# A GNN layer with experts followed by graph attention on one core: the MoE rounds run in teams of two groups of nodes instead of four, and the rows of x are fetched between the rounds, kept in memory and loaded back

## The chip, the core and the metric

The kernel runs on one core of a Trainium2 chip. The metric is the device time of one launch in microseconds (us); lower is better. One profiled execution shows what every engine did: TensorE (PE, with its weight loads as PEld), VectorE (DVE), ScalarE (ACT), GpSimd (POOL) and SyncE (SP), and the transfers of the DMA queues.

## The reference

The graph has 6250 nodes with 128 features (x) and 106,250 directed edges (50,000 pairs in both directions, and a self loop for each node). Everything is float32.

```
h = x @ W_in + b_in                                        # 6250 x 256
for l in 0, 1, 2:
    agg    = mean of h[src] over the edges that end in the node
    logits = [h, agg] @ router_W[l] + router_b[l]          # 8 experts
    gates  = softmax over the two largest logits, 0 elsewhere
    weak   = relu(agg @ weak_W[l][e] + weak_b[l][e])       # 4 experts, 256 -> 256
    strong = relu(agg @ W1[l][e] + b1) @ W2[l][e] + b2     # 4 experts, 256 -> 512 -> 256
    h      = h + sigmoid(h @ conf_W[l] + conf_b[l]) * sum_e gates[e] * expert_e
x = layernorm(x + h @ W_out + b_out)
y = elu(gat(x, 4 heads of 32)); x = layernorm(x + gat(y, 1 head of 128))
```

A gat layer adds up the rows of the neighbours with softmax weights that come from one score of the source and one of the destination for each head.

## The kernel before, in words

**Stages.** The kernel first sorts the nodes by degree, puts them into 49 groups of 128, computes h and gathers it in that order (up to about 330 us). Then come the three MoE rounds, then the normalised x is stored as the table for the first attention layer, and two attention layers follow. The change touches the three rounds, what lies between them, and the end of the sorting.

**Gathers.** In each round GpSimd issues 800 indirect gathers (`hidden_rows`, L589), each of 128 rows of h out of the round's table `hidden_tab[r]` in memory, one row for each node of a group. They go into a ring of 32 slots, which is used as 8 units of 4 slots. Before the third gather of a unit GpSimd waits until VectorE has freed the next unit (`ring_free`). SyncE loads the lists of row numbers for 32 gathers ahead (`stage`, L404 to L426) and tells VectorE unit by unit what has arrived (`tell`, L408 to L415).

**VectorE.** `aggregate(r, q, j)` (L875 to L901) adds up the units of group j of team q: it multiplies the first unit into the accumulator (L880), adds whole units (L886), adds the last one (L890), the node's own row and the sum over the four parts, and writes the mean into the team's aggregate (L901). For the first group of a team this write waits until TensorE has turned the aggregate of the team before (`tr_ready`), since there is one such buffer. A team is `TEAM` = 4 groups: 12 teams and a last one with a single group, 13 in all (`BATCHES`). VectorE's step of a team is an order written out by hand: the next team's aggregates one by one, and between them `rank_experts` (top two and what the exponential needs), `weigh_experts` (L957 on, the gates), and the adding of weak and strong experts to h (`add_weak`, L930; `add_strong`, L921).

**TensorE.** Its step of a team is written out too (`step` below): turn the aggregate (`turn_agg`, transposes), the router's product, computed as logits by nodes and turned back (`router`, `turn_logits`, L1668), the first layer of the strong experts (`strong_first`, L1677, four chunks of 128 outputs each, 512 columns for four groups), the weak experts of one group (L1687 with the bias, L1689), the second strong layer (`second`, L1700 with the bias, L1702, 256 columns for each group), and so on for the four experts and groups. The last second layer of a team comes at the start of the next team's step. In round 2 each step also turns the finished state of the team before and multiplies it by W_out (`turn_state`, `project`). At the start of each round a pass of 13 batches turns h and makes the part of the logits that depends on h itself (`own_turn`, `own_logits`, L1629 and L1640).

**ScalarE** copies the turned aggregate, does the relus (L1343) and the exponential (`gate_exp`, L1334), scales weak and strong results by the gates (L1364, L1352), and issues the store of a finished team's h into the next round's table (`keep_state`, L1376). The next round's first gather waits for all these stores (`table_done`).

**Weights.** One set of buffers serves all rounds. SyncE issues the loads of a round (L440 to L445) after it has told of the first 32 gathers of the round and when the second layers of the round before have ended; TensorE waits for `s_wts` ahead of the first step.

**x.** After the gathers of round 2 GpSimd fetches the 49 groups of x into a part of the ring (L626), when the ring is free. VectorE adds them to the projected state (`residual`, L986 to L993), takes the variances (L998), and ScalarE copies the turned result for the attention tables (L1451).

**Compaction.** At the end of the sorting the neighbours' numbers of each group are copied to their place in one list, group after group: VectorE one group (L841), ScalarE the next (L1293), in turn. SyncE stores the list (`slot_tab`) and loads its first 32 columns (L426); then GpSimd starts the first round (it waits for the list at L577).

## Time and profile before

| | us |
|---|---|
| runs | 5852.50, 5852.51, 5859.92; median 5852.51 |
| profiled execution, its own time | 5857.3 |
| its span | 5855.7 |
| GpSimd busy | 4188.6 (72%) |
| VectorE busy | 3452.8 (59%) |
| TensorE busy | 3218.5 (55%) |
| ScalarE busy | 1199.8 (20%) |
| sorting, h, up to the first gather | 330 |
| MoE rounds 0, 1, 2, first to last gather | 1017, 1015, 1037 |
| last gather of a round to the first of the next stage | 91, 89, 142 |
| rest: two attention layers and the output | 2134 |

The busy times are shares of the whole span. The stages differ in what limits them, so a share of 72% says little about any one of them; the rows below are read stage by stage.

### The profile page before, as it was taken

To read this page: it belongs to the slowest core of one execution; us is meant where nothing else is said; L and a number is where in the kernel's file an instruction comes from. 1 tells how busy PE (TensorE), PEld (TensorE's weight loads), DVE (VectorE), ACT (ScalarE), POOL (GpSimd) and SP (SyncE) were. 2 spreads that over 40 slices of the span, in tenths; PEclk is the share of its full clock that TensorE was granted. 3 is DMA by queue.
4 is the path that set the end of the run, shared out by engine and by line. 5 is a ranking of instruction groups with operands and counts; after the bars stand their busy time and mean duration, and the time that the engine had idled before them with its cause. 6 is when DMAs were issued, how large, how long until landed. Compare 5 with 4: busy or idle time off the path is not lost.

```text
span 5855.7 us, 59691 instructions
## 1 busy us (share of the span) xinstructions
PE 3218.5 (55%) x11995; PEld 2032.2 (35%) x11995; DVE 3452.8 (59%) x6754; ACT 1199.8 (20%) x2737; POOL 4188.6 (72%) x4323
## 2 busy tenths in 40 slices
PE   4068889999879899989899999200000000000000
PEld 3055555556545555565465566200000000000000
DVE  5337667674556666636566665555555556556563
ACT  1022223333223233323233333200000000000000
POOL 7777777772777777547777766477777767777777
PEclk8569999999889999979999999655555555555555
DMA  4144443441443333333333332223222222222221
GB/s 111 51 147 109 112 112 106 111 110 50 141 111 112 108 111 110 87 107 104 102 102 100 102 95 70 54 59 60 59 60 59 59 46 56 55 55 55 56 55 50
DMA packets 248524, 500.35 MB, mean 85 GB/s; under 512 B 103196, under 2 KB 132437, under 8 KB 248037
## 3 DMA queue, kind: packets, MB, share of 16 engines
q0 software_dynamic: 176592, 446.04, 29.5%
q1 hardware_dynamic: 55226, 33.55, 2.2%
q10 hardware_dynamic: 16608, 19.67, 1.0%
q8 instruction: 36, 0.59, 0.0%
q14 instruction: 62, 0.50, 0.0%
HBM read 464.23 MB, written 34.72 MB: 85 GB/s over the span
## 4 chain that ended last, share of the span: by engine, by line
POOL 25%; PE 24%; issue 15%; DVE 13%; DVEq 12%; DMA 6%; ACT 2%; ACTq 0%; POOLq 0%; SPq 0%
POOL ring L589 22%; PE ps_w1a L1677 5%; PE ps_w1b L1677 4%; PE ps_gate L1702 4%; PE ps_wide L1702 3%; DMA ring<-gat_tab,stage 3%; DVE ps_wide L1135 3%; PE ps_weak_a L1689 2%; PE ps_weak_b L1689 2%; DMA ring<-hidden_tab,stage 2%; DVEq L1167 2%; DVEq L883 1%; DVE ps_wide L930 1%; DVEq L1177 1%; DVEq L1180 1%
## 5 line engine op out<-in xcount | busy, mean ns | idle before, releaser
L589 POOL DMA_INDIRECT ring<-hidden_tab,stage x2400 | 2304.8, 960 | 954.4 <-issue 891.1
L589 POOL DMA_INDIRECT ring<-gat_tab,stage x1600 | 1543.6, 965 | 585.9 <-issue 545.1
L886 DVE TENSOR_TENSOR ps_wide<-ps_wide,ring 128x1024 f32<-128x1024 f32 x450 | 560.2, 1245 | 208.7 <-SPq L415 124.6
L1677 PE MATMUL ps_w1a<-agg_team_t,wbuf 128*128 128x512 f32 (+1 forms) x1248 | 562.2, 573 | 7.3 <-ACT strong L1343 5.9
L1702 PE MATMUL ps_gate<-wbuf,strong 128*128 128x256 f32 x2400 | 560.0, 380 | 0.0
L1677 PE MATMUL ps_w1b<-agg_team_t,wbuf 128*128 128x512 f32 (+1 forms) x1248 | 556.1, 568 | 0.0
L1807 PE MATMUL ps_w1a<-ident,agg_team_t 128*128 128x128 f32 x28 | 7.8, 434 | 995.9 <-DVE agg_team_t L1213 995.9
L1702 PE MATMUL ps_wide<-wbuf,strong 128*128 128x256 f32 x2304 | 537.3, 380 | 0.0
L1702 PEld LDWEIGHTS ps_gate<-wbuf,strong 128*128 128x128 f32 x2400 | 433.3, 191 | 110.6 <-issue 47.7
L1702 PEld LDWEIGHTS ps_wide<-wbuf,strong 128*128 128x128 f32 x2304 | 416.0, 191 | 77.9
L1495 ACT ACTIVATE ps_gate<-shifted 128x36 f32<-128x36 f32 x296 | 60.4, 204 | 1862.4 <-DVEq L1124 1849.1
L1141 DVE TENSOR_REDUCE h_res<-ps_wide 128x1188 f32 (+1 forms) x296 | 411.0, 1388 | 0.1
L930 DVE TENSOR_REDUCE ps_wide<-weak 128x256 f32<-128x1024 f32 x147 | 285.0, 1939 | 185.1 <-ACT weak L1364 171.6
L1135 DVE TENSOR_TENSOR ps_wide<-ring,ps_gate 128x1056 f32<-128x1056 f32 x296 | 372.9, 1260 | 0.0
L1343 ACT ACTIVATE strong<-ps_w1a,b_t 128x512 f32<-128x512 f32 (+1 forms) x312 | 206.7, 663 | 748.2 <-PE ps_w1a L1677 748.2
L1807 PEld LDWEIGHTS ps_w1a<-ident,agg_team_t 128*128 128x128 f32 x28 | 5.0, 217 | 998.0 <-DVE agg_team_t L1213 998.0
L890 DVE SCALAR_TENSOR_TENSOR ps_wide<-ring,before_cut,ps_wide 128x256 f32<-128x256 f32 x588 | 244.6, 485 | 174.8 <-SPq L415 136.3
L1677 PEld LDWEIGHTS ps_w1a<-agg_team_t,wbuf 128*128 128x128 f32 x1248 | 230.1, 191 | 306.3 <-issue 296.2
L1677 PEld LDWEIGHTS ps_w1b<-agg_team_t,wbuf 128*128 128x128 f32 x1248 | 231.9, 190 | 275.1 <-issue 275.1
L1107 DVE TENSOR_TENSOR score<-ring,h_res 128x32 f32 (+1 forms) x296 | 57.0, 193 | 443.0 <-SPq L419 386.2
L1689 PE MATMUL ps_weak_a<-wbuf,agg_team_t 128*128 128x512 f32 x588 | 289.1, 616 | 0.0
L1689 PE MATMUL ps_weak_b<-wbuf,agg_team_t 128*128 128x512 f32 x588 | 279.8, 599 | 0.0
(356 smaller groups left out, 4578.3 us busy)
## 6 DMA issues: line engine op xcount, KB each, us to landing
ring<-hidden_tab,stage POOLq DMA_INDIRECT x2400, 2.8
ring<-gat_tab,stage POOLq DMA_INDIRECT x1600, 2.6
hidden_tab<-h_res ACTq DMA_DIRECT2D x24, 512.0 KB, 3.0
hidden_tab<-h_res SPq DMA_DIRECT2D x12, 512.0 KB, 8.5
wbuf<-in_L_gnn_strong_W SPq DMA_DIRECT2D x6, 1024.0 KB, 9.5
wbuf<-in_L_gnn_strong_W SPq DMA_DIRECT2D x12, 512.0 KB, 14.3
gat_tab<-h_res ACTq DMA_DIRECT2D x7, 476.0 KB, 3.7
gat_tab<-h_res ACTq DMA_DIRECT2D x12, 272.0 KB, 2.4
```

Of the source, the lines that this page charges most:

```text
L589: return pool.indirect_dma_start(out=ring[:, b, 0:width], out_offset=None, in_=table, in_offset=bass.IndirectOffsetOnAxis(ap=stage[:, half ...
L886: nc.vector.tensor_tensor(wide_s, wide_s, rows(u), ALU.add).then_inc(ring_free, 1)
L890: nc.vector.scalar_tensor_tensor(wide_s[:, b, :], slot(last, b), before_cut[:, bass.ds(g + 1, 1), b:b + 1].rearrange("p a s -> p (a s)"), ...
L930: nc.vector.tensor_reduce(wide[:, 0:H], weak[j % 2][:].rearrange("p e n -> p n e"), AX.X, ALU.add)\
L1135: last = nc.vector.tensor_tensor(terms[:, 0:GSLOTS, :, :], rows_of(unit)[:, :, 0:HEADS * HC].rearrange("p s (h c) -> p s h c", c=HC), p[:, ...
L1141: nc.vector.tensor_reduce(sums(g), terms.rearrange("p s h c -> p (h c) s"), AX.X, ALU.add)
L1167: dve.drain()
L1343: nc.scalar.activation(strong[s % 2][:, c, 0:size * P], ps_w1[c % 2][:, 0:size * P], ACT.Relu, bias=b1_t[:, k:k + 1]).then_inc(relu_ready, 1)
L1495: nc.scalar.activation(ps_gate[:, 0:(GSLOTS + 1) * HEADS], shifted[:].rearrange("p s h -> p (s h)"), ACT.Exp).then_inc(p_ready, 1)
L1677: last = mm(ps_w1[c % 2][:, 0:size * P], w1_w[:, k, s, c * P:(c + 1) * P], agg_team_t[:, k, 0:size * P], start=k == 0, stop=k == 1)
L1689: last = mm(ps_weak[x][:], agg_team_t[:, k, j * P:(j + 1) * P], wk_w[:, k, x * 512:(x + 1) * 512], start=False, stop=k == 1)
L1702: last = mm(o, strong[s % 2][:, c, j * P:(j + 1) * P], w2_w[:, c, s, :], start=False, stop=c == 3)
```

## The change

- `TEAM` goes from 4 to 2: 24 teams and a last one with a single group, 25 turns. The batches of four stay for the projected state's residuals, the tables and the first pass of own logits. The rooms in SBUF and PSUM are cut anew: four buffers for the first layer's output (one for each strong expert) in place of two, two chunks of the first layer in one PSUM bank, and the state of the finished team in the upper half of `scaled_d`.
- The orders of a step on TensorE, VectorE and ScalarE are written anew. The exponential of the gates now stands on ScalarE behind all the relus of the team.
- The router's logits are made directly by nodes, with no turning back. Its bias comes in with the own logits by a product with a row of ones.
- The next round's own logits are made within the step, from the finished state of the team before (`turn_state` and `project` run in every round: logits in rounds 0 and 1, W_out in round 2). The pass of 13 batches stays ahead of round 0 alone and starts group by group as h lands.
- x is fetched by GpSimd in the passages: 32 groups after round 0, 17 after round 1. SyncE stores them in a table `x_tab` in five pieces, GpSimd waits for the stores before the next round's gathers, and SyncE loads all five pieces back into the ring after round 2.
- The compaction is done by VectorE alone with a drain behind each group.
- The bias parts in bf16 are computed across 128 partitions and brought into their rows through a table in memory; GpSimd no longer waits for them.

The core of the diff (left out are the counting of semaphores by turns instead of batches, the views of the new rooms, the helpers that follow the team's size, the bias parts and the first pass of own logits):

```
+X_PIECES = ((0, 8), (8, 20), (20, 32), (32, 44), (44, 49))
...
-TEAM = 4
+BATCHES = -(-GROUPS // BATCH)
+TEAM = 2
 TEAMS = GROUPS // TEAM
-BATCHES = TEAMS + 1
-STORES = 2 * BATCHES + BATCHES
+TURNS = TEAMS + 1
+PAIRS = 2
+STORES = 2 * TURNS + BATCHES
...
-EARLY = (TEAMS - 1) * TEAM
+EARLY = (BATCHES - 2) * BATCH
...
-strong = [sb(f"strong{i}", [P, 4, TEAM * P]) for i in range(2)]
+strong_room = sb("strong_room", [P, NS, 4, TEAM * P])
+strong = [strong_room[:, s, :, :] for s in range(NS)]
...
-scaled_d = sb("scaled_d", [P, TEAM, H])
-scaled = [scaled_a, scaled_b, scaled_c, scaled_d]
+scaled_d = sb("scaled_d", [P, BATCH, H])
+scaled = [scaled_a, scaled_b, scaled_c, scaled_d[:, 0:TEAM, :]]
+state_now = scaled_d[:, TEAM:2 * TEAM, :]
...
         if r == 1:
             keep_places(bodies - 1, bass.ds((bodies - 1) % 2 * RING, RING))
             sp.wait_ge(places_kept, bodies * 16 + 16)
+        if r in (1, 2):
+            for a, b in (X_PIECES[0:3], X_PIECES[3:])[r - 1]:
+                if a == 0:
+                    sp.wait_ge(ggathered[GUNITS - 1], 16 * GSLOTS)
+                else:
+                    sp.wait_ge(x_landed[(a - GSLOTS) // (3 * BATCH)], 16 * (b - a))
+                sp.dma_start(x_tab[:, a:b, :], x_ring[:, a:b, :]).then_inc(x_stored, 16)
+        if r == LAYERS:
+            sp.wait_ge(ring_free, bodies * (UNITS * LAYERS) + UNITS)
+            for c, (a, b) in enumerate(X_PIECES):
+                sp.dma_start(x_ring[:, a:b, :], x_tab[:, a:b, :]).then_inc(x_back[c], 16)
...
-    pool.wait_ge(s_strong_parts, 16 * len(PART_ROWS))
...
-        if r == LAYERS - 1:
-            pool.wait_ge(ring_free, bodies * (UNITS * LAYERS) + UNITS)
+        if r < 2:
+            pool.wait_ge(ring_free, bodies * (UNITS * (r + 1)) + UNITS)
             pool.sem_inc(half_begun, 1)
-            pool.wait_ge(agg_ready, LAYERS * BATCHES)
-            for g in range(GROUPS):
+            for g in (range(0, 32), range(32, GROUPS))[r]:
                 pool.indirect_dma_start(out=x_ring[:, g, :], out_offset=None, in_=x,
                                         in_offset=bass.IndirectOffsetOnAxis(ap=perm[:, g, 0:1], axis=0))\
-                    .then_inc(ggathered[GUNITS - 1] if g < GSLOTS else x_landed[(g - GSLOTS) // (3 * TEAM)], 16)
+                    .then_inc(ggathered[GUNITS - 1] if g < GSLOTS else x_landed[(g - GSLOTS) // (3 * BATCH)], 16)
+        if r < 2:
+            pool.wait_ge(x_stored, 16 * (3, len(X_PIECES))[r])
         if r < LAYERS - 1:
-            pool.wait_ge(table_done, 16 * BATCHES * (r + 1))
+            pool.wait_ge(table_done, 16 * TURNS * (r + 1))
...
     dve.wait_ge(s_blanked, 16)
-    def compact(g):
+    with dve.Fori(0, GROUPS) as g:
         at = dve.value_load(cum_at[0:1, bass.ds(g, 1)], min_val=0, max_val=COLS - RUN)
-        dve.wait_ge(s_compact, g + 1)
-        nc.vector.tensor_scalar(slots_sb[:, bass.ds(at, RUN)], run_raw[:, bass.ds(g, 1), :].rearrange("p a k -> p (a k)"),
-                                0.0, None, ALU.add).then_inc(s_compact, 1)
-    with dve.Fori(0, GROUPS // 2) as i:
-        compact(i * 2)
-    compact(GROUPS - 1)
+        nc.vector.tensor_scalar(slots_sb[:, bass.ds(at, RUN)], run_raw[:, bass.ds(g, 1), :].rearrange("p a k -> p (a k)"), 0.0, None, ALU.add)
+        dve.drain()
     dve.drain().then_inc(s_slots, 1)
...
         if j == 0:
-            w(dve, tr_ready, n * 2)
-        return nc.vector.tensor_scalar(agg4[:, j, :], part[:], rdeg[:, bass.ds(g, 1)], None, ALU.mult)
+            w(dve, tr_ready, n)
+        return nc.vector.tensor_scalar(agg_now[:, j, :], part[:], rdeg[:, bass.ds(g, 1)], None, ALU.mult)
...
-        if b < 2:
-            dve.wait_ge(ggathered[GUNITS - 1], 16 * GSLOTS)
-        else:
-            dve.wait_ge(x_landed[(b - 2) // 3], 16 * (3 * BATCH if b < TEAMS - 1 else 1 + BATCH))
-        dve.wait_ge(z_ready, b + 1)
+        dve.wait_ge(x_back[0 if b < 2 else min(1 + (b - 2) // 3, 4)], 16)
+        dve.wait_ge(z_ready, min((b + 1) * BATCH // TEAM, TURNS))
...
-            def between():
-                if r == LAYERS - 1 and spare:
-                    residual(spare.pop(0))
+            def between(count):
+                if r == LAYERS - 1:
+                    for _ in range(min(count, len(spare))):
+                        residual(spare.pop(0))
             spare = list(meanwhile)
             gather_next(0)
             if after == 1:
                 fill_up(r)
             if tail:
-                add_strong(r, q - 1, NS - 1, TEAM)
+                add_weak(r, q - 1, TEAM - 1, TEAM)
+                add_strong(r, q - 1, 2, TEAM)
+                add_strong(r, q - 1, 3, TEAM)
             rank_experts(r, q, size)
             weigh_experts(r, q, size)
+            between(2 if size == 1 else 0)
+            gather_next(1)
             add_weak(r, q, 0, size)
-            for s in range(1, NS):
-                gather_next(s)
-                between()
-                add_strong(r, q, s - 1, size)
-                between()
-                if s < size:
-                    dve.drain()
-                    add_weak(r, q, s, size)
+            add_strong(r, q, 0, size)
+            between(2 if size == 1 else 0)
+            add_strong(r, q, 1, size)
+            between(1)
         for j in range(TEAM):
             done = aggregate(r, 0, j)
...
         step(0, TEAM, TEAM, False)
         with dve.Fori(1, TEAMS - 1) as q:
             step(q, TEAM, TEAM)
-        step(TEAMS - 1, TEAM, 1, meanwhile=range(0, 6))
-        step(TEAMS, 1, 0, meanwhile=range(6, TEAMS))
+        step(TEAMS - 1, TEAM, 1, meanwhile=range(0, 1))
+        step(TEAMS, 1, 0, meanwhile=range(1, 6))
+        add_strong(r, TEAMS, 2, 1)
         if r == LAYERS - 1:
+            residual(6)
+        add_strong(r, TEAMS, 3, 1)
+        if r == LAYERS - 1:
+            for b in range(7, BATCHES - 1):
+                residual(b)
             variances(0, EARLY)
-        add_strong(r, TEAMS, NS - 1, 1)
...
-    act.wait_ge(s_cum, 1)
-    with act.Fori(0, GROUPS // 2) as i:
-        at = act.value_load(cum_at[0:1, bass.ds(i * 2 + 1, 1)], min_val=0, max_val=COLS - RUN)
-        act.wait_ge(s_compact, i * 2 + 2)
-        nc.scalar.activation(slots_sb[:, bass.ds(at, RUN)], run_raw[:, bass.ds(i * 2 + 1, 1), :].rearrange("p a k -> p (a k)"),
-                             ACT.Copy).then_inc(s_compact, 1)
...
-        def step(q, size, after, tail=True):
+        def step(q, size, tail=True):
             if tail:
-                scale_strong(r, q - 1, TEAM, NS - 1)
-            for k in range(2):
-                take_agg_t(r, q, size, k)
-            logits_t(r, q, size)
-            relu(r, q, size, 0)
+                scale_strong(r, q - 1, TEAM, 2)
+            take_agg_t(r, q, size)
+            if tail:
+                scale_strong(r, q - 1, TEAM, 3)
             logits(r, q, size)
-            relu(r, q, size, 1)
+            for s in range(NS):
+                relu(r, q, size, s)
             gate_exp(r, q, size)
             weak_relu(r, q, size, 0)
             scale_strong(r, q, size, 0)
-            if tail and r == LAYERS - 1:
+            if tail:
                 take_state(r, q - 1, TEAM)
-            elif tail:
-                keep_state(r, q - 1, TEAM)
-            relu(r, q, size, 2)
+                if r < LAYERS - 1:
+                    keep_state(r, q - 1, TEAM)
+            scale_strong(r, q, size, 1)
+            if tail:
+                take_state_t(r, q - 1, TEAM)
             if size > 1:
                 weak_relu(r, q, size, 1)
-            scale_strong(r, q, size, 1)
-            if tail and r == LAYERS - 1:
-                take_state_t(q - 1, TEAM)
-            relu(r, q, size, 3)
-            if size > 1:
-                weak_relu(r, q, size, 2)
-            scale_strong(r, q, size, 2)
-            if tail and r == LAYERS - 1:
-                take_z(q - 1, TEAM)
-            if size > 1:
-                weak_relu(r, q, size, 3)
+            if tail:
+                take_projected(r, q - 1, TEAM)
...
-        pe.wait_ge(lgT_copied, q + (r * BATCHES + 1))
+        n = q + r * TURNS
+        w(pe, weak_copied, n * (2 * TEAM))
+        pe.wait_ge(tr_copied, n + 1)
         for j in range(size):
-            last = mm(ps_weak[1][:, j * 16:j * 16 + NE + 1], logit_t[:, j * P:(j + 1) * P], ident[0:NE + 1, 0:NE + 1], start=True, stop=True)
+            for k in range(2):
+                last = mm(ps_weak[1][:, j * 16:j * 16 + NE + 1], agg_team_t[:, k, j * P:(j + 1) * P], rt_w[:, r, 2 + k, :], start=k == 0, stop=k == 1)
         last.then_inc(logits_ready, 1)
...
-        def step(q, size, after, tail=True):
-            projects = tail and r == LAYERS - 1
+        def step(q, size, tail=True):
+            relus = (q + r * TURNS) * (NS * PAIRS) + NS * PAIRS
             if tail:
-                second(r, q - 1, TEAM, NS - 1)
+                second(r, q - 1, TEAM, 2)
             turn_agg(r, q, size)
+            if tail:
+                second(r, q - 1, TEAM, 3)
             router(r, q, size)
             strong_first(r, q, size, 0)
-            turn_logits(r, q, size)
+            strong_first(r, q, size, 1)
             weak_experts(r, q, size, 0)
-            for s in range(1, NS):
-                if s == NS - 1 and projects:
-                    pe.wait_ge(houtT_copied, q * 2)
-                strong_first(r, q, size, s)
-                second(r, q, size, s - 1)
-                if s == 2 and projects:
-                    turn_state(q, q - 1, TEAM, 12)
-                if s == NS - 1 and projects:
-                    pe.wait_ge(relu_ready, q * 16 + (r * BATCHES * 16 + 16))
-                    project(q - 1, TEAM)
-                if s < size:
-                    weak_experts(r, q, size, s)
-            if projects:
-                pe.wait_ge(z_ready, q)
-        if r:
-            pe.wait_ge(relu_ready, r * BATCHES * 16)
-            pe.wait_ge(weak_copied, r * BATCHES * 8)
-            pe.wait_ge(mo_copied, r * BATCHES * 2 * NS)
-        own_turn(r, 0)
-        for q in range(BATCHES):
-            if q + 1 < BATCHES:
-                own_turn(r, q + 1)
-            own_logits(r, q)
-        pe.wait_ge(own_copied, 2 * BATCHES * (r + 1))
-        pe.wait_ge(own_taken, BATCHES * (r + 1))
+            strong_first(r, q, size, 2)
+            strong_first(r, q, size, 3)
+            second(r, q, size, 0)
+            second(r, q, size, 1)
+            if tail:
+                turn_state(r, q - 1, TEAM, relus - 1)
+            if size > 1:
+                weak_experts(r, q, size, 1)
+            if tail:
+                project(r, q - 1, TEAM, relus)
+        if r == 0:
+            own_turn(0)
+            for q in range(BATCHES):
+                if q + 1 < BATCHES:
+                    own_turn(q + 1)
+                own_logits(q)
+            pe.wait_ge(own_copied, 2 * BATCHES)
+            pe.wait_ge(own_taken, BATCHES)
```

## Rows read from the trace of the kernel before

**Rows 1.** Stretches: length, busy us of PE, PEld, DVE, ACT, POOL, PEclk, DMA, GB/s

```profile
330.00:1347.00 1017.00, 933.78 (x3269) 573.34 (x3270) 678.45 (x1335) 303.97 (x627) 767.52 (x800) 0.93 0.43 115
1438.00:2453.00 1015.00, 919.65 (x3265) 562.12 (x3265) 645.03 (x1136) 303.17 (x627) 767.52 (x800) 0.93 0.40 114
2542.00:3579.00 1037.00, 973.17 (x3591) 609.62 (x3591) 644.26 (x1136) 328.61 (x667) 769.22 (x800) 0.95 0.37 107
```

**Rows 2.** Timeline of GpSimd: start, us, engine, line, operation, tiles [idle before <-releaser]

```profile
329.67 0.94 POOL L589 DMA_INDIRECT ring<-hidden_tab,stage  x1 [9.78 <-issue]
...
1437.95 0.94 POOL L589 DMA_INDIRECT ring<-hidden_tab,stage  x1 [90.90 <-issue]
...
3578.16 0.95 POOL L589 DMA_INDIRECT ring<-hidden_tab,stage  x1 [0.30 <-issue]
...
3721.37 0.94 POOL L589 DMA_INDIRECT ring<-gat_tab,stage  x1 [69.42 <-issue]
```

**Rows 3.** Waits of GpSimd, 2584 to 3579: us in total, times, longest

```profile
POOL ring L589 <- DVE ps_wide L880: 29.2, 16, 6.6
```

**Rows 4.** Timeline of TensorE, first team of round 1

```profile
1518.99 0.39 PE L1687 MATMUL ps_weak_a<-wk_parts,even_rows 128*128 128x512 bf16 x1
...
1522.86 1.88 PE L1677 MATMUL ps_w1a<-agg_team_t,wbuf 128*128 128x512 f32 x4
1524.58 0.59 PE L1677 MATMUL ps_w1b<-agg_team_t,wbuf 128*128 128x512 f32 x1
...
1529.73 0.27 PE L1700 MATMUL ps_gate<-wk_parts,odd_rows 128*128 128x256 bf16 x1
1529.84 1.89 PE L1702 MATMUL ps_gate<-wbuf,strong 128*128 128x256 f32 x8
1531.57 0.27 PE L1700 MATMUL ps_gate<-wk_parts,odd_rows 128*128 128x256 bf16 x1
```

**Rows 5.** Timeline of VectorE, first team of round 1

```profile
1468.34 0.35 DVE L901 TENSOR_SCALAR x_res<-part,rdeg 128x256 f32<-128x256 f32 x1
...
1530.75 0.17 DVE L957 TENSOR_SCALAR gate_n<-ex 128x8 f32<-128x8 f32 x1 [9.63 <-ACT ex L1334]
```

**Rows 6.** Timeline of SyncE's queue, weights of round 1

```profile
1482.00 9.70 SPq L445 DMA_DIRECT2D wbuf<-in_L_gnn_strong_W  x4
```

**Rows 7.** DMA issues, 1436 to 1600: KB each, median us to landing

```profile
wbuf<-in_L_gnn_strong_W SPq DMA_DIRECT2D x4, 512.0 KB, 13.6
wbuf<-in_L_gnn_weak_W SPq DMA_DIRECT2D x2, 512.0 KB, 6.4
```

**Rows 8.** Timeline of VectorE, end of round 0 and passage

```profile
1353.78 0.35 DVE L901 TENSOR_SCALAR x_res<-part,rdeg 128x256 f32<-128x256 f32 x1
...
1434.30 0.42 DVE L921 TENSOR_TENSOR h_res<-h_res,scaled_d 128x256 f32<-128x256 f32 x1 [2.31 <-ACT scaled_d L1352]
```

**Rows 9.** Timeline of ScalarE, first and last passage

```profile
1434.80 0.35 ACTq L1376 DMA_DIRECT2D hidden_tab<-h_res  x1
...
3685.60 0.60 ACT L1451 ACTIVATE h_team_t<-ps_wide 128x512 f32<-128x512 f32 x1 [1.33 <-PE ps_wide L1783]
```

**Rows 10.** Timeline of VectorE, last passage

```profile
3664.49 0.69 DVE L986 TENSOR_TENSOR ring<-h_res,ring 128x512 f32<-128x512 f32 x1
...
3666.90 0.66 DVE L986 TENSOR_TENSOR ring<-h_res,ring 128x512 f32<-128x512 f32 x1
...
3677.10 0.19 DVE L998 TENSOR_SCALAR ln_r<-ln_mv 128x44 f32<-128x44 f32 x1
```

**Rows 11.** Timeline of VectorE, compaction

```profile
281.83 0.20 DVE L841 TENSOR_SCALAR wbuf<-wbuf  x1 [1.20 <-ACT wbuf L1293]
```

**Rows 12.** Timeline of SyncE's queue, end of the sorting

```profile
316.02 0.34 SPq L426 DMA_DIRECT2D stage<-slot_tab  x1
```

**Rows 13.** Two more stretches, columns as in rows 1

```profile
1483.00:1507.00 24.00, 1.11 (x6) 1.04 (x7) 9.78 (x17) 0.38 (x2) 18.21 (x20) 0.50 0.92 308
1507.00:1511.00 4.00, 4.00 (x13) 1.66 (x11) 2.38 (x6) 1.19 (x2) 3.09 (x4) 0.66 0.41 113
```

327 lines of the change are left out of this document (167 added, 160 removed).

## The prediction

> **What bounds the kernel now.** I read the busy times stretch by stretch first [rows 1]. In the three MoE rounds GpSimd issues 800 gathers (its count in each row) in 1017, 1015 and 1037 us. Then its own timeline [rows 2]: a gather is 0.95 us of work with 0.30 idle ahead, so 800 need 1000 us, and some 15 us of longer single issues come on top. The rounds run at GpSimd's pace, and the rest of its time is start and passages: idle 90.90 us from round 0 to 1 [rows 2], 89 us from 1 to 2 (2453 to 2542, the bounds of the stretches in [rows 1]), and 142 us from the last gather of round 2 (3578.16 + 0.95) to the first of the attention (3721.37) [rows 2], in which it also issues the 49 gathers of x. Round 2 lost 29.2 - 16 x 0.3 = 24 us to ring slots that VectorE had not freed [rows 3]. TensorE is nearly full as well: 934 of 1017 us [rows 1].
>
> **TensorE per step.** Prices at the full clock [rows 4]: a 4-matmul chunk pair of the first strong layer 1.72 us at 512 columns (1522.86 to 1524.58); a group of the second layer 1.84 (1529.73 to 1531.57), all of 256 columns; a group of weak experts 3.87 (1518.99 to 1522.86). The new first layer has 256 columns. The second layer shows that 256 columns keep pace: (1.84 - 0.11)/8 = 0.216 us for an instruction, against 1.72/4 = 0.43 for 512. So the work per column stays: first layers 4 x 3.46 = 13.8, second layers 4 x 3.68 = 14.7, weak 7.7. I put 0.11 on each small instruction: two turns of 4 transposes 0.9, router 8 x 0.11 = 0.9, the next round's own logits 10 x 0.11 = 1.1. A step of two groups is 39.2 us. The gathers give it 1015 x 2/49 = 41.4 us, so GpSimd remains the slower, by 2.2 us a step. Teams differ (a group fills 2 to 8 of the ring units of four gathers, 5 us each): light ones leave TensorE late, by my running sum of 39.2 against their gathers up to 13 us, heavy ones give it back. VectorE frees the first unit of a team's second group some 30 us after TensorE's turn of the team before (exponential at 24.2, gates 1.8, start of the group 4), while the ring lets gathers run 7.5 units ahead; for a first group of u units the gathers stall only if that turn is later than 5u - 3.5 us after its operand, 11.5 us for u = 3 and 16.5 for u = 4. For the steady part I take 0; bounds -5 and the +79 of rival 1.
>
> **The start of a round, the costly part.** Team 0 used to be complete with its fourth group. With two groups it is complete at 1468.7 [rows 5], 31 us after the round's first gather at 1437.95. But SyncE issues the weights only after the first 32 gathers have landed: the four of W2 take 1482.00 to 1491.70 [rows 6] and land 13.6 us after issue [rows 7], so near 1504, 66 us into the round. Nothing of this moves. What follows, in us from the round's first gather:
> - VectorE computes group 2 and then waits to write it, since the one aggregate buffer is read by TensorE's turn: until 67.
> - Softmax's exponential stands on ScalarE behind all four relus (it stood behind two; even so VectorE waited 9.63 us for it [rows 5]). Turn, copy and router take 4 us at the low clock, two first layers 6.9, a weak group 3.9, two more first layers 6.9: exponential at 89, gates at 91, group 3's first unit consumed at 94.
> - Until then 7 ring units are free again (2 + 2 + 3 units of the groups 0 to 2), which with the 8 of the ring lets gathers go on to the middle of unit 14, number 58: 58 x 1.25 = 72.5. GpSimd stands from 72.5 to 94: **22 us**.
> - Team 1's gates come at 103.6 + 24.2 + 1.8 = 129.6, its next unit is freed at 133, against gather 86 at 107.5 + 22: 3 to 4 us more. Later teams are inside the 16.5 us.
> So 26 us in each round, 78 in all; bounds 5 a round (weights landing some 15 us sooner) and 35 (two more teams stalled).
>
> **Round 2** paid for projection on top and lost the 24 us above. The new step costs nearly the same in all rounds, so round 2 goes back to its neighbours': 1037 - 1016: **-20** (0 to -23), the start-up stall being counted already.
>
> **The passages between rounds.** The last full team had four groups; its work (78 us) and the last single group's (25 us) set the end: last add at 1434.30 [rows 8], store at 1434.80 [rows 9], first gather at 1437.95. The new chain, from the last group's aggregate at 1353.78 + 0.35 [rows 8], which comes with the gathers and does not move: pending adds 3.6, ranking and gates 3.7 -> 1361.4; weak relus, first scaling, copy of the state 3.2 -> 1364.6; turn, weak group 3.87, own logits -> 1370.2; second layer 3.68, turn of group 48, second layer 3.68, router -> 1378.3; two first layers 4.3, weak 3.87, two first layers 4.2, relu, exponential -> 1391.7; gates, weak relus, scaling, copy -> 1396.2; turn, copy, own logits -> 1398.9; two second layers 3.7 -> 1402.6; scale, add, copy -> 1404.8 store, +3.15 as before -> 1408. So **-30**; for 1 to 2 likewise **-28**. Bounds 15 and 40 for each.
> What is late next is the x chain: 32 gathers from 1355.5 need 40 us, +2.5 landing, and a store of 768 KB. No row has this store; a weight load of 512 KB took 6.4 us [rows 7], which brings 1405: 3 us inside; by the longest row, 13.6, it would be 1412, 4 us more. The 17 gathers of the second passage need 21 us. SyncE's further loads queue behind these stores, but are needed only 32 gathers later.
>
> **The last passage.** The x gathers leave; five loads from memory follow once the ring is free (about 3588) and land long before use. VectorE's twelve residual batches stay: 2.41 us each (3664.49 to 3666.90 [rows 10]). Placed as written, one runs before the last gates (which I put at 3625.8), eleven after them: 11 x 2.35 = 25.9, with the adds 4.8 -> variances at 3656.5 against 3677.10 [rows 10]. From there all is unchanged, save that the state's last projection (4 us) no longer comes in between. ScalarE's first operand copy at 3685.60 [rows 9] comes at 3662.3: **-23** (-10 to -35).
>
> **The prologue.** The compaction of 49 groups goes from VectorE and ScalarE in turn to VectorE alone with a drain each. Before, the 0.20 us copy stood 1.20 us idle for ScalarE's, so a pair took about 1.4 [rows 11], and 24.5 pairs 34; alone a group costs the 0.20 us, a register load and loop control, which I estimate at 0.95 together, between half the pair (0.7, nothing lost) and a whole one (1.4), nearer to the low end because the handoff to ScalarE goes. 49 x 0.95 = 46.6, so the end moves from 312 to 325 or, with the loop's first and last pass, 327. The load of the first stage follows 4 us after it: at 316.02 before [rows 12], at 331 now. Before, GpSimd's own work let the first gather start only at 329.67 [rows 2]; now the load is last, and with 2.5 us of landing it is 333.6. So **+4** (0 to +20). The added small loads at the start and three bias stores and loads end long before SyncE and VectorE have the next thing GpSimd waits for; 0. The 13 batches of own logits at each round start went beside gathers; 0, both ways.
>
> **Sum**, against the profiled execution (span 5855.7, time 5857.3): +4 + 78 - 20 - 30 - 28 - 23 = -19, 5838. The median of the runs, 5852.5, is 4.8 lower, so **5834**. This kernel's runs differ by 0.1%, and 0.2% (12 us) is about what a measurement tells from no change.
>
> **Rivals.**
> 1. *TensorE becomes the bound* (slower). Place: the handoffs turn - copy - router and gates - weak relu - turn of the state, twice as many now. It decides from 41.4 us a step, 2.2 above my sum. At 42.5 each of 72 steps loses 1.1: +79, 5913. For it: 934 of 1017 us busy now [rows 1]. Against: a second layer is put behind the turn, where TensorE waited. Chance 0.15.
> 2. *The clock.* While TensorE idled from 1483 to 1507 the granted clock was 0.50, i.e. 1.2 GHz [rows 13], and after a heavy team it would restart there. In the 4 us after the restart its mean was 0.66 [rows 13], 1.4 us lost. The turn of the state waits for the gates in every step that starts on time: 31.7 us after the turn of the aggregate, where TensorE comes at 30.3. If each step has that wait and a restart, it is 39.2 + 1.4 + 1.4 = 42.0, and 72 x 0.6 = 43, with half of round 2's stalls kept: 5887. It decides from the same 41.4. Chance 0.10. [...]
> 3. *No start-up stall*: weights ready earlier, or VectorE not held; 5 in place of 26 a round, 5771. Against it: the counted ring units. Chance 0.15.
> 4. *The passages are handoffs, not team size*: both chains shrink half as far and the x stores bind: +43, 5877. Chance 0.12.
>
> **Numbers.** Forecast 0.48, own range 5805 to 5862, of it 0.35 faster, 0.11 same, 0.02 slower. With rival 3 (faster), rival 2 and 4 (0.06 of them same, the rest slower), rival 1 slower: faster 0.50, same 0.18, slower 0.32. Range 5775 to 5912: the low end takes in most of rival 3, the high end rivals 2 and 4 and half of rival 1.
>
> **What would show it.** GpSimd idle of about 22 us after gather 58 of each MoE round, released by VectorE's L880; passages near 61, 60 and 119 us; no x gather in the last; no other stall over 5 us in rounds. Wrong if TensorE never idles in mid-round, if passages exceed 75 us, or if the gathers of a round's start run through.

## The result and the profile after

The changed kernel takes 5876.7 us (median of 7 runs, 5871.36 to 5880.76) against 5855.27 (7 runs) for the kernel before on the same chip: 1.0037 times as long, 95% interval 1.0027 to 1.0047. It is 0.4% slower, where 0.3% faster was forecast; the time lies inside the stated range. The profiled execution has a span of 5873.8 us, 18.1 more than before. The stages of the two traces, from the start of a round's first gather to the end of its last:

| | before | forecast | after | difference |
|---|---|---|---|---|
| first gather of round 0 | 329.7 | +4 | 332.9 | +3.2 |
| round 0 | 1017.4 | +26 | 1058.0 | +40.6 |
| passage 0 to 1 | 90.8 | -30 | 61.3 | -29.5 |
| round 1 | 1014.9 | +26 | 1052.5 | +37.6 |
| passage 1 to 2 | 89.2 | -28 | 64.4 | -24.8 |
| round 2 | 1037.1 | +26 - 20 | 1058.3 | +21.2 |
| last passage | 142.3 | -23 | 114.5 | -27.8 |
| attention and output | 2134.3 | 0 | 2131.9 | -2.4 |
| span | 5855.7 | -19 | 5873.8 | +18.1 |

So the passages came as forecast and the rounds did not. The three rounds after, as stretches with the columns of [rows 1]:

```profile
333.00:1391.00 1058.00, 932.86 (x4215) 724.16 (x4216) 707.03 (x1544) 350.85 (x879) 770.43 (x800) 0.94 0.42 111
1452.00:2505.00 1053.00, 931.67 (x4234) 725.46 (x4235) 678.00 (x1347) 352.23 (x881) 769.17 (x800) 0.94 0.38 110
...
2569.00:3628.00 1059.00, 948.09 (x4278) 735.38 (x4279) 677.66 (x1347) 355.69 (x881) 769.57 (x800) 0.94 0.36 104
```

The 800 gathers cost the same 770 us of work. TensorE is about as busy as before (933, 932 and 948 us against 934, 920 and 973) and runs at the same mean clock, 0.94. The time is idle time of GpSimd. Its timeline shows each stop (the columns of [rows 2]):

```profile
332.93 0.95 POOL L610 DMA_INDIRECT ring<-hidden_tab,stage  x1 [39.77 <-DMA stage<-slot_tab]
...
1452.19 0.94 POOL L610 DMA_INDIRECT ring<-hidden_tab,stage  x1 [12.49 <-issue]
...
1546.73 0.95 POOL L610 DMA_INDIRECT ring<-hidden_tab,stage  x1 [22.41 <-DVE ps_wide L899]
...
1585.18 0.94 POOL L610 DMA_INDIRECT ring<-hidden_tab,stage  x1 [3.45 <-DVE ps_wide L899]
...
1893.35 0.94 POOL L610 DMA_INDIRECT ring<-hidden_tab,stage  x1 [3.58 <-DVE ps_wide L899]
...
2396.84 0.94 POOL L610 DMA_INDIRECT ring<-hidden_tab,stage  x1 [3.61 <-DVE ps_wide L899]
...
3741.94 0.95 POOL L610 DMA_INDIRECT ring<-gat_tab,stage  x1 [114.50 <-issue]
```

L899 is the old L880, the multiply of a group's first unit that frees it. The stop at 1546.73 stands behind gather 58 of round 1, where it was forecast, and the one at 1585.18 behind gather 86. In the three rounds the first is 22.9, 22.4 and 21.9 us, the second 6.6, 3.4 and 3.0. The later ones (behind gathers 326, 494, 686 and 714 of every round, 2.7 to 4.4 us each) were forecast not to be there; with all stops over 1 us, less the usual 0.3 each, they come to 15, 13 and 20 us a round. Of the first chain this is the trace of round 1, weights on SyncE, then TensorE, then VectorE:

```profile
1496.05 9.97 SPq L466 DMA_DIRECT2D wbuf<-in_L_gnn_strong_W  x4
```

```profile
1516.29 1.11 PE L1659 MATMUL ps_w1a<-ident,x_res 128*128 128x128 f32 x4 [64.61 <-DMA wbuf<-in_L_gnn_strong_W]
```

```profile
1482.51 0.35 DVE L920 TENSOR_SCALAR x_res<-part,rdeg 128x256 f32<-128x256 f32 x1
...
1517.45 0.35 DVE L920 TENSOR_SCALAR x_res<-part,rdeg 128x256 f32<-128x256 f32 x1 [20.06 <-PE ps_w1a L1659]
...
1540.96 0.17 DVE L976 TENSOR_SCALAR gate_n<-ex 128x4 f32<-128x4 f32 x1 [19.14 <-ACT ex L1343]
...
1544.28 1.65 DVE L899 TENSOR_SCALAR ps_wide<-ring,from_cur 128x256 f32 x4 [0.36 <-issue]
```

Team 0 is complete at 1482.9, TensorE's first turn waits for the weights until 1516.3, VectorE stands 20 us to write group 2 and 19 us for the exponential, and frees the unit at 1544.3 plus 1.65: each link is the forecast's.

### The profile page after: what moved, and what is told of

Read it like the earlier page. It is cut to its first block, busy times and chain, and to the rows that moved or that the text cites. A ratio compares the mean times of both kernels' runs of the same rounds, so it can differ in the third digit from the quotient of the medians.

```text
span 5873.8 us, 67923 instructions
## 1 busy us (share of the span) xinstructions
PE 3172.2 (54%) x14563; PEld 2480.5 (42%) x14563; DVE 3499.6 (60%) x7377; ACT 1297.5 (22%) x3413; POOL 4156.4 (71%) x4324
## 4 chain that ended last, share of the span: by engine, by line
PE 26%; POOL 24%; issue 15%; DVE 12%; DVEq 11%; DMA 6%; ACT 1%; SPq 1%; ACTq 0%; POOLq 0%
POOL ring L610 22%; PE ps_w1a L1680 5%; PE ps_w1b L1680 5%; PE ps_wide L1705 4%; PE ps_gate L1705 4%; DMA ring<-gat_tab,stage 3%; DVE ps_wide L1158 3%; PE ps_weak_a L1693 3%; PE ps_weak_b L1693 2%; DVEq L902 1%; DMA ring<-hidden_tab,stage 1%; DVEq L1190 1%; DVE ps_wide L949 1%; DVEq L1203 1%; DVEq L1200 1%
## 5 line engine op out<-in xcount | busy, mean ns | idle before, releaser
L1680 PE MATMUL ps_w1a<-agg_team_t,wbuf 128*128 128x256 f32 (+1 forms) x2400 | 568.9, 380 | 0.0
L1705 PE MATMUL ps_wide<-wbuf,strong_room 128*128 128x256 f32 x2352 | 560.7, 385 | 0.0
L1680 PE MATMUL ps_w1b<-agg_team_t,wbuf 128*128 128x256 f32 (+1 forms) x2400 | 557.4, 375 | 0.0
L1705 PE MATMUL ps_gate<-wbuf,strong_room 128*128 128x256 f32 x2352 | 552.0, 381 | 0.0
L1680 PEld LDWEIGHTS ps_w1a<-agg_team_t,wbuf 128*128 128x128 f32 x2400 | 447.6, 192 | 89.5 <-issue 35.9
L1680 PEld LDWEIGHTS ps_w1b<-agg_team_t,wbuf 128*128 128x128 f32 x2400 | 450.1, 190 | 59.8
L1705 PEld LDWEIGHTS ps_wide<-wbuf,strong_room 128*128 128x128 f32 x2352 | 432.5, 194 | 76.5 <-issue 1.7
L1705 PEld LDWEIGHTS ps_gate<-wbuf,strong_room 128*128 128x128 f32 x2352 | 426.3, 191 | 73.2 <-issue 1.0
L1354 ACT ACTIVATE strong_room<-ps_w1a,b_t 128x256 f32<-128x256 f32 x600 | 248.8, 466 | 607.1 <-PE ps_w1a L1680 607.1
L1354 ACT ACTIVATE strong_room<-ps_w1b,b_t 128x256 f32<-128x256 f32 x600 | 248.9, 466 | 258.3 <-PE ps_w1b L1680 258.3
```

What stands on the lines that cost most here:

```text
L1354: last = nc.scalar.activation(strong[s][:, c, 0:size * P], ps_w1[pair][:, half * TEAM * P:half * TEAM * P + size * P], ACT.Relu, bias=b1_t ...
L1680: last = mm(ps_w1[pair][:, half * TEAM * P:half * TEAM * P + size * P], w1_w[:, k, s, c * P:(c + 1) * P], agg_team_t[:, k, 0:size * P], st ...
L1705: last = mm(o, strong[s][:, c, j * P:(j + 1) * P], w2_w[:, c, s, :], start=False, stop=c == 3)
```

## The experiments

Two theories of the start: S, late weights hold it, against B (the slack only moves to later teams) and O (not the weights). Two of mid-round: P, TensorE's pace, against E, the place of the exponential. Two of the last passage: H, the smaller team shortened it, against X, moving x did.

**A disturbed chip.** Four kernels, edits by name (the diffs stand with the runs that could be read).

`e1_weights_early`: 

> SyncE issues a round's weights ahead of its second stage load and of telling of the first 32 gathers, instead of behind both. Theory S (the late weights make the stall at the start of a round): the stalls after gather 58 (22 us) and 86 (3 to 7 us) go in all three rounds, TensorE's first turn comes within 1 us of team 0's aggregate, each round is 25 to 29 us shorter, 5877 becomes 5800. Rival B (the budget moves): TensorE has only about 2 us to spare in a step, so the start's stall covered part of later ones; the stalls at 58 and 86 go but others of 5 to 15 us a round grow after heavy teams, 5820 to 5845. Rival O (one aggregate buffer or the exponential is the cause, not the weights): a stall of over 10 us stays near gather 58, 5850 or more.

`e2_exp_third`: 

> ScalarE does the exponential of the gates behind the relus of the third strong expert instead of the fourth, so up to 3.5 us earlier in a step. Theory E (the stalls of 3 to 4 us after gathers 326, 494, 686, 714 come from the exponential's place): these stalls shrink by 3 us each and the stall after 58 by 3 us, 10 to 15 us a round, 5877 becomes 5840 to 5850. Rival P (TensorE's pace makes them): with TensorE as late as before, at most 3 us a round are gained at 58, and where VectorE ranks late the fourth relus wait behind the exponential and TensorE loses what is gained; 5865 to 5880.

`e3_less_tensor`: 

> In rounds 0 and 1 the turn of the finished state is one transpose in place of four and the next round's own logits are the bias row's product alone, nine or ten small matmuls fewer; round 2 is as it was. It leaves out the part of the router's logits and of the confidence that comes from h in rounds 1 and 2. TensorE's step falls from 39.4 to about 38 us in rounds 0 and 1. Theory P (TensorE's pace makes the stalls in mid-round): the stalls behind gather 100 fall from 13 to 15 us to under 6 in rounds 0 and 1 and stay at 17 to 20 in round 2; 5877 becomes 5860. Theory E (the exponential's place): they stay at 10 or more in every round, 5870 to 5877. The stall after 58 stays in both.

`e4_x_last_compact_both`: 

> Two parts undone in two stages that the profile tells apart: GpSimd fetches all 49 groups of x after round 2, with no table for x; and the compaction is shared by VectorE and ScalarE again. Theory H (the x stores are hidden in the passages between rounds, and the last passage got shorter by the smaller team): passages after rounds 0 and 1 stay at 61 and 64 us within 2, the last passage goes from 114.5 to 118 to 125. Rival X (moving x made the gain of the last passage): it goes back to 135 or more; or the x stores hold the passages, which then fall by 3 or more. Compaction: the first gather comes at 329.5 in place of 332.9 if the drain for each group costs it, unchanged if not. Total 5877 to 5885 under H, 5895 under X.

They took 8244.8, 8238.5, 8188.0 and 8262.6 us, and so did the kernel before: 8236 (31 runs). The effects looked for are at most 1.3%, and single executions differ there by up to 2%, so none of the totals tells anything of the theories. The same again on another chip:

`e5_weights_early_again`: 

> The kernel of the early weights once more, since on the chip of the first call all kernels, the one before the change too, took 8.2 ms, with ScalarE and TensorE standing 7 to 20 us at a time for something that no engine of this core released; that hides every difference looked for. On a chip where the kernel before takes 5855: theory S 5800, with no stall after gathers 58 and 86; rival B 5820 to 5845; rival O 5850 or more.

8291 against 8262. On a third chip with the same trouble (the kernel before 8226, 31 runs) came three of them once more and a combination:

`e7_exp_third_again`: 

> The exponential of the gates behind the third strong expert's relus, again, for a chip on which the kernel before takes 5855. Theory E: the stalls after gathers 326, 494, 686 and 714 shrink by 3 us each and the one after 58 by 3 us, 10 to 15 us a round, 5877 becomes 5835 to 5850. Rival P (TensorE's pace makes them): at most 3 us a round, at gather 58; 5865 to 5880.

`e8_less_tensor_again`: 

> Fewer matmuls for the finished state in rounds 0 and 1, round 2 as it was (it leaves out the part of the router's logits and of the confidence that comes from h in rounds 1 and 2), again, for a chip like that of the prediction. TensorE's step 39.4 becomes about 38. Theory P: stalls behind gather 100 fall from 13 to 15 us to under 6 in rounds 0 and 1 and stay at 17 to 20 in round 2; 5860. Theory E: they stay at 10 or more in every round; 5870 to 5877.

`e9_x_last_compact_both_again`: 

> All 49 groups of x fetched after round 2, and the compaction shared by VectorE and ScalarE, again, for a chip like that of the prediction. Theory H: passages after rounds 0 and 1 stay at 61 and 64 us within 2, the last passage goes from 114.5 to 118 to 125. Rival X: it goes back to 135 or more, or the first two fall by 3 or more. Compaction: first gather at 329.5 in place of 332.9 if the drain for each group costs it. Total 5877 to 5885 under H, 5895 under X.

`e10_early_third_shared`: 

> Three edits together: weights early (5800 by itself), the exponential behind the third expert's relus, the compaction shared. If their effects add: theory E 5755 to 5770, since 10 to 15 us a round of stalls are left in mid-round and 3 us come from the compaction; rival P 5790 to 5800.

8217, 8189, 8251 and 8220: inconclusive as well. What these chips did is told at the end. All that follows is from chips on which the kernel before takes 5849 to 5861.

**Weights early.** SyncE's order at the start of each round:

```
-                    load(1, 1)
-                    tell(0)
                     if r:
                         sp.wait_ge(w2_ready, r * TURNS * NS)
                     for k in range(2):
...
+                    load(1, 1)
+                    tell(0)
                     load(2, 0)
```

> The kernel of the early weights a third time, for a chip on which the kernel before takes about 5855. On the chips of the first two calls ScalarE stood 17 to 33 us at the first instruction of nearly each pass of its loop over the teams, and TensorE 12 to 23 us, with nothing of this core to wait for. If the chip is like the one of the prediction: theory S 5800, with no stall after gathers 58 and 86; rival B 5820 to 5845; rival O 5850 or more. If it is like the others: 8.2 ms again.

Measured: 5800.14 us, 0.9914 of the kernel before (0.9885 to 0.9943). Theory S said 5800. In this kernel's timeline of SyncE the four loads of W2 for round 1 are issued from 6 us ahead of that round's first gather (1423.5), where they came 44 us behind it:

```profile
1417.51 7.25 SPq L464 DMA_DIRECT2D wbuf<-in_L_gnn_strong_W  x4
```

The stops behind gathers 58 and 86 are gone in all rounds, which take 1028.5, 1026.4 and 1032.7 us: 29.5, 26.1 and 25.6 less. Rivals B and O fall: the stops of mid-round in round 0 are the old ones to 0.1 us (3.0, 3.0, 2.7, 3.1), so nothing moved to later teams. The passages lost 3.4 and 3.8 us of this (64.7, 68.2): the last store of h, issued 1 us behind the weights, now takes 6.0 us to land in place of 1.7.

**One edit a round.** To read several theories from one execution:

```
                     for s in range(NS):
                         relu(r, q, size, s)
-                    gate_exp(r, q, size)
+                        if s == (3, 2, 1)[r]:
+                            gate_exp(r, q, size)
...
-                for k in range(2):
-                    for j in range(size):
+                for k in range(2 if r else 1):
+                    for j in range(size if r else 1):
...
-                    state_logits(ps_w1[1], state_t, r + 1, size).then_inc(b_out_ready, 1)
+                    if r:
+                        state_logits(ps_w1[1], state_t, r + 1, size).then_inc(b_out_ready, 1)
+                    else:
+                        mm(ps_w1[1][:, 0:size * 16], ones_row[:], rt_bias[...], start=True, stop=True).then_inc(b_out_ready, 1)
...
-                if r < 2:
+                if r == LAYERS - 1:
...
-                    for g in (range(0, 32), range(32, GROUPS))[r]:
+                    for g in range(GROUPS):
```

together with the early weights, no stores and loads of `x_tab`, the old waits of `residual` for x, and the old compaction.

> On top of the early weights one edit in each stage, to be read stage by stage against the early-weights kernel of 5800 (rounds 1028.5, 1026.4, 1032.7 us, of which stalls of over 1 us 14.8, 12.7, 18.1; passages 64.7, 68.2, 114.4). Round 0: fewer matmuls for the finished state (it leaves out what h gives to the router's logits and the confidence of round 1). Round 1: exponential behind the third expert's relus. Round 2: exponential behind the second expert's. x fetched wholly after round 2. Compaction shared again. Theory P (TensorE's pace makes the stalls in mid-round): round 0 falls to stalls under 6, rounds 1 and 2 stay at 10 and 15 or more. Theory E (the exponential's place): round 0 stays at 10 or more, round 1 falls to under 4, round 2 to under 6. Passages, theory H: the first two stay within 2 or lose the 3.5 us that the early weights brought, the last goes to 118 to 125; rival X: 135 or more. First gather at 329 or 330 either way.

Measured: 5752.7 us. Read by stage, first the waits of GpSimd behind the start of the round (us in total, times, longest), for round 0 of the early-weights kernel and of this one:

```profile
POOL ring L610 <- DVE ps_wide L899: 21.2, 21, 3.1
```

```profile
POOL ring L600 <- DVE ps_wide L893: 10.2, 16, 1.8
```

- *Round 0, fewer matmuls.* No stop over 2 us is left behind gather 100, where four were. As theory P said. The round as a whole is longer all the same, 1036.5 in place of 1028.5, since with the earlier first gather it stops 12.8 us behind gather 58 and 4.3 behind 86 (why, see the next run).
- *Round 1, exponential third.* Stops over 1 us 4.8 us in place of 12.7, the round 1018.8 in place of 1026.4. As theory E said, though not under 4.
- *Round 2, exponential second.* 8.4 in place of 18.1, 1020.8 in place of 1032.7. As E said, though not under 6.

P and E were wrongly put as rivals: both edits shorten one and the same chain (turn, router, relus, exponential, gates, first unit freed), at different links. Fewer matmuls bring the turn forward: TensorE's step falls from 39.4 to 38.1 us, and the turn of team 8 stands 22.4 us behind its last gather's landing in place of 26.1. The exponential behind the third relus leaves the turns where they were (24.9 against 25.0) and frees the unit 25.6 us behind a turn in place of 29.1. Behind the second it frees it 18.2 us behind the turn in place of 28.9, but the turns come 6 us later (34.3 against 28.0), which eats most of the gain. Some 4 us off the chain take most of the stops away, because they are only 3 to 4 us long.

- *Passages.* 63.7, 63.5 and 115.1, against 64.7, 68.2 and 114.4 with x moved. H holds, and more: moving x gained nothing in the last passage. Nor did it hold the first two: in the changed kernel the last store of x lands at 1445.3, 6 us ahead of the last store of h (1451.0), and in the early-weights kernel 10 and 32 us ahead. Of the 1 and 5 us by which these passages are shorter here, the last store of h comes 1.2 and 2.7 us sooner, by this run's other edits; in the second some 2 us between that store's landing and the first gather went with x. The last store of x in the changed kernel (KB, us to landing):

```profile
x_tab<-ring SPq DMA_DIRECT2D x1, 768.0 KB, 3.9
```
- *The start.* The first gather comes at 301.2, not at 329 or 330. Neither theory had that.

**All four edits.** Weights early, exponential behind the third expert's relus in every round, x after round 2, the old compaction; the whole computation.

> The whole computation again, with the four edits that the stage readings favour: weights early, exponential behind the third expert's relus in all rounds, compaction shared, x fetched after round 2. If the gains of the stages add: first gather at 301, round 0 with a start-up stall of 17 us (the 13 batches of own logits now end behind the first aggregate) and under 6 in mid-round, 1030 to 1037; rounds 1 and 2 at 1019 and 1022; passages 64, 64, 115; 5750 to 5760 in all. If the third place of the exponential helps round 2 less than the second did: round 2 at 1027 or more, 5760 to 5765. 8.2 ms if the chip is one of the disturbed ones.

Measured: 5738.96 us, 0.9804 of the kernel before (0.9788 to 0.9821) and some 137 less than the changed kernel: the version that beats both. Its rounds (columns of [rows 1]):

```profile
301.50:1331.00 1029.50, 982.76 (x4447) 774.52 (x4447) 708.10 (x1545) 359.56 (x907) 768.78 (x800) 0.95 0.42 114
1394.00:2411.00 1017.00, 931.57 (x4228) 725.22 (x4229) 680.01 (x1347) 350.67 (x881) 767.95 (x800) 0.96 0.39 112
2474.00:3495.00 1021.00, 945.32 (x4267) 733.76 (x4268) 677.86 (x1347) 354.83 (x881) 767.62 (x800) 0.96 0.37 106
```

By the first and last gather they take 1028.9, 1016.7 and 1020.8 us. Rounds 1 and 2 are those of one edit a round within 2.1 us, so the third place serves round 2 as well as the second. In round 0 a start-up stop of 9.6 and 3.0 us is left (17 expected): TensorE is busy with the 13 batches of own logits until 355.6, at a granted clock of 0.50, and turns team 0 at 355.9, 27 us behind its last gather's landing.

**What the start consists of.** The prologue came out at +3.2 against +4, and yet the old compaction alone brought 30 us. In the changed kernel VectorE's first and last copy of the compaction are

```profile
254.80 0.20 DVE L864 TENSOR_SCALAR wbuf<-wbuf  x1 [1.45 <-issue]
256.33 0.20 DVE L864 TENSOR_SCALAR wbuf<-wbuf  x1 [1.34 <-issue]
...
325.73 0.20 DVE L864 TENSOR_SCALAR wbuf<-wbuf  x1 [1.26 <-issue]
```

71 us, 1.48 from one group to the next; a shared pair takes 1.3, 32 us in all. And the compaction begins 26 us earlier than before. By itself:

```
-            with dve.Fori(0, GROUPS) as g:
-                at = dve.value_load(...)
-                nc.vector.tensor_scalar(slots_sb[...], run_raw[...], 0.0, None, ALU.add)
-                dve.drain()
...
+            with dve.Fori(0, GROUPS // 2) as i:
+                compact(i * 2)
+            compact(GROUPS - 1)
```

with ScalarE's half as before.

> The changed kernel (5877) with the compaction shared by VectorE and ScalarE again and nothing else. The compaction takes 32 us in place of 71 and the first gather comes at 301 to 304 in place of 332.9. From there all is as in the changed kernel, but the weights of round 0 still come 66 us after the first gather: 5877 - 30 = 5847, if the gain of the start is kept to the end; 5860 or more if it is lost to the first round.

Measured: first gather at 300.4, 5843.97 us, 0.9981 of the kernel before (0.9970 to 0.9992). By the medians all of the 33 us are kept to the end (the profiled execution, 5.7 us above its median, keeps 26); with the compaction left alone the change would have been faster by 0.2%.

For the earlier start: before, VectorE made the bias parts in one partition while GpSimd fetched the source rows. The kernel before at that place, GpSimd and VectorE:

```profile
140.46 4.94 POOL L522 DMA_INDIRECT wbuf<-in_src,wbuf  x1 [0.31 <-issue]
145.71 3.32 POOL L522 DMA_INDIRECT wbuf<-in_src,wbuf  x1 [0.30 <-DMA wbuf<-in_src,wbuf]
```

```profile
140.11 3.35 DVE L685 TENSOR_TENSOR ring<-ring,wk_parts 1x3072 f32<-1x3072 f32 x1
143.53 1.75 DVE L687 CAST wk_parts<-ring 1x3072 bf16<-1x3072 f32 x1
145.40 3.51 DVE L682 CAST ring<-ring 1x3072 bf16<-1x3072 f32 x2
```

A gather, elsewhere 0.95 us, takes 4.94 there and ends just behind VectorE's cast; the next takes 3.32 and ends with the casts after it. The old work was put back into the kernel of all four edits as dummy work, at its old place, on an unused part of the ring:

```
             dve.drain().then_inc(s_meta, 1)
+            for i in range(2):
...
+                for nth, row in enumerate(PART_ROWS):
...
+                        nc.vector.tensor_copy(part_of, rest)
+                    for _ in range(nth):
...
+                            nc.vector.tensor_tensor(rest, rest, part_of, ALU.subtract)
...
+                            nc.vector.tensor_copy(part_of, rest)
```

That makes 12 casts and 6 subtractions.

> The kernel of all four edits (5739) with VectorE's old bias work put back as dummy work at its old place, 12 casts and 6 subtractions of 3072 columns in one partition of the ring, just when GpSimd gathers the source rows. Theory G (VectorE's work slows GpSimd's gathers): those gathers take 2 to 5 us in place of 0.95 while it lasts, the 49 of them 81 us of work in place of 52, the first gather of round 0 comes 26 us later, at about 328, 5739 becomes 5765. Rival N (it was the earlier start of something else, since VectorE itself waits for GpSimd's chain there): first gather unchanged at 302, 5740.

> Only the 12 casts of that work (1.75 us each, 21 us). If the casts are what locks GpSimd out: gathers of over 2 us as long as they last and a first gather 15 to 21 us later than 301.5. If it is the subtractions: unchanged within 3.

> Only the 6 subtractions with both inputs in SBUF (3.35 us each, 20 us). If they block the gathers too: first gather 15 to 20 us later; if only the casts do: within 3 of 301.5.

The source gathers (busy us, mean ns, idle) without it, with all of it, with the casts alone, with the subtractions alone:

```profile
L534 POOL DMA_INDIRECT wbuf<-in_src,wbuf x49 | 52.3, 1068 | 14.9 <-issue 14.9
```

```profile
L534 POOL DMA_INDIRECT wbuf<-in_src,wbuf x49 | 81.6, 1665 | 14.9 <-issue 14.6 <-DMA wbuf<-in_src,wbuf 0.3
```

```profile
L534 POOL DMA_INDIRECT wbuf<-in_src,wbuf x49 | 66.7, 1360 | 14.9 <-issue 14.9
```

```profile
L534 POOL DMA_INDIRECT wbuf<-in_src,wbuf x49 | 68.0, 1388 | 14.9 <-issue 14.6 <-DMA wbuf<-in_src,wbuf 0.3
```

First gathers at 301.5, 330.9, 317.5 and 317.0; totals 5739.0, 5769.5, 5754.2 and 5757.1. Theory G holds, and casts and subtractions block alike. Rival N (an earlier start of something else) falls: all of the old start, 329.7, is back within 1.2 us.

## Why the prediction was wrong, point by point

- **The start of a round**: right. Gather 58 and 22 us, then 3 to 4 us behind gather 86, in every round (the 6.6 of round 0 apart). The early weights took away 29, 26 and 26 us of the rounds, which is the term's 26.
- **The passages**: right, 61.3, 64.4 and 114.5 against 61, 60 and 119. That moving x has no part in the gain is shown. What is left of the change there is the smaller team with its new orders; no run takes these two apart. The forecast had the store of x land 3 us ahead of need in the first passage; it was 6.
- **The steady part: the step that failed.** "For the steady part I take 0." The step of TensorE was right: 39.4 us from turn to turn in rounds 0 and 1 where it never idles (39.2 forecast). So was VectorE's freeing of a unit some 30 us behind a turn. The lateness of the turn was not: "by my running sum ... up to 13 us". Measured in round 1, team 20, its last gather and its turn:

```profile
2334.99 0.95 POOL L610 DMA_INDIRECT ring<-hidden_tab,stage  x1 [0.30 <-issue]
```

```profile
2366.98 0.60 PE L1659 MATMUL ps_w1a<-ident,x_res 128*128 128x128 f32 x4
```

  The gather landed 2.8 us behind its issue's end, at 2338.7, and the turn is 28.2 us later. VectorE needs 3.6 of these for the aggregate (the turn of team 5, for which TensorE stood ready, is 3.6 behind), so in the prediction's terms it is 25 us late. The sum left out what a heavy team leaves behind. When VectorE waits for the gathers of the next team's first group, everything it does for the team before waits too: the last unit of group 12, one of eight, is added from 1758.84, and so ScalarE stands 22 us ahead of the exponential of team 5, and TensorE in the middle of its step, with 10 us of it still to do (VectorE, ScalarE, TensorE):

```profile
1758.84 1.66 DVE L909 SCALAR_TENSOR_TENSOR ps_wide<-ring,before_cut,ps_wide 128x256 f32<-128x256 f32 x4 [4.58 <-SPq L425]
...
1768.97 0.20 ACT L1343 ACTIVATE ex<-ex_in 128x4 f32<-128x4 f32 x1 [22.13 <-DVEq L968]
...
1774.09 1.11 PE L1714 MATMUL ps_w1a<-ident,scaled_d 128*128 128x128 f32 x4 [20.78 <-ACT scaled_d L1381]
...
1784.79 0.60 PE L1659 MATMUL ps_w1a<-ident,x_res 128*128 128x128 f32 x4
```

  So TensorE begins a run of light teams 12 us late already (team 6, behind its landing), and is 25 late two teams on: the 13 us of the running sum come on top of the 12. Before, with teams of four, no turn within round 1 was more than 20 us behind its landing; in round 2 they were up to 24, and there GpSimd did stall [rows 3]. Against its own threshold (11.5 us for a group of three units, 16.5 for four) even 13 should have cost something; I set it aside. It cost 12 us in rounds 0 and 1. The bounds (-5 to +79) held it. That this lateness is what costs is read from the trace, and both edits that shorten the chain behind it took the stops away; no run took away the wait in mid-step itself.
- **Round 2, -20**: the same step again. The projection's stalls of [rows 3] did go, but round 2 has the new ones, and most of all of them (20 us, since its step is 40.1 us). 1058.3 less the start's 24.3 is 1034.0, so -3 in place of -20. The two steps together are +21 where -20 stood, 41 us; all the other terms together are 4 us off the other way.
- **The prologue**: right in sum, wrong in both terms. A group of the compaction costs 1.48 us alone, not 0.95, and more than the estimate's upper bound of 1.4: 71 us in place of 46.6, which holds the first gather back by 32.5 us (300.4 to 332.9). The bias parts, put at "0", bring GpSimd's own chain forward by 29.3 (329.7 to 300.4). A forecast that meets the sum proves none of its terms.
- **The rivals.** TensorE as the bound (rival 1) is the nearest: not by the length of the step, which is at most 40.1 where TensorE waits for nothing, but by its lateness behind heavy teams. The clock (rival 2) did not fall: the granted mean is 0.94 in each round, 0.93 to 0.95 before [rows 1], with all first layers at 256 columns; eight such matmuls take 1.73 us where they follow each other. In the 160 us of light teams of round 1 in which TensorE never idles it is 1.00:

```profile
1800.00:1960.00 160.00, 159.55 (x737) 124.72 (x736) 111.27 (x227) 60.59 (x152) 118.70 (x124) 1.00 0.37 108
```

  The wait for the turn of the state, with the restart behind it, did not come in each step but three times behind heavy teams in round 1 (20.8, 15.5 and 7.7 us). Rival 3 did not come. Rival 4 names 5877 us, which is what was measured, but by luck: its 43 us are longer passages, and these came as forecast.
- **The signs.** None of the three signs of being wrong came, and the stops in mid-round stay under the 5 us that were allowed; the time moved the other way even so. Small stops have to be summed over a round to tell. By their own terms the chances of faster, same and slower add up to 0.50, 0.17 and 0.33, not 0.50, 0.18 and 0.32.

## What to carry to other kernels

Where one engine runs ahead through a ring, measure how late the consumer is against the landing of the data, not against the engine that hands it over, and start the running sum of light stretches from what the heavy one before leaves undone: a wait in mid-step costs the rest of the step. Put loads that need nothing but a free buffer ahead of waits on the same queue; here that one order on SyncE was worth some 75 us. And ask of work on VectorE that nobody waits for what GpSimd does meanwhile.

## What was not expected of the hardware

- VectorE's casts and its subtractions with both inputs in SBUF, in one partition, hold up GpSimd's indirect gathers until they end: 2.0 to 4.9 us in place of 0.95 (above), 29 us in all, with no wait in the trace between the two engines. The Trainium skill, "SBUF — State Buffer", section "SBUF: two separate sides", has the rule: VectorE and GpSimd share a pair of ports under an exclusive lock, and while VectorE holds it in its two-port modes a DMA issued by GpSimd can't write its descriptors. It names copies and casts for this. Of an operation with two inputs in SBUF it says that it holds up a GpSimd operation that reads SBUF, and that in a probe `tensor_tensor` did not stall a DMA; to the gathers here the subtractions alone do the same as the casts (first gather 15.5 us later against 16).
- In the three sets of runs at the start every kernel took 8.2 ms; the attention layers are longer there too, some 2620 us in place of 2132. It is not a fixed trait of a chip: the third set ran on chip 15, and on a chip of that number the kernel before took 5853 us nine minutes later. ScalarE stood there above all at the first instruction of its loop over the teams, the scaling at L1363, with nothing of this core to release it. Its waits in 1000 us of round 1 of the early-weights kernel, us in total, times, longest:

```profile
ACT x_res L1363 <- remote: 269.6, 11, 32.9
...
ACT strong_room L1354 <- remote: 88.1, 7, 18.1
ACT scaled_d L1363 <- remote: 69.5, 6, 22.0
```

  The longest come back once in each pass of the loop, mostly 38 instructions apart on ScalarE and 182 on TensorE; where the kernel before took 5849 us, the same kernel shows none. The Trainium skill, "Runtime: NRT & Kernel Launch", section "Instruction fetch mechanics", says that a taken branch out of the loaded window waits for its code. That fits the place, does not say why it came only there, and was not tried: the cause stays open. The shared compaction gained there about what it gained here (first gather at 376 in place of 413), but x fetched after round 2 cost 54 us in the last passage (180 in place of 126) and gained about 30 and 9 in the two others: what moving x is worth depends on such a disturbance.
